# The triangular solver of a delta-rule layer on GpSimd instead of VectorE, with its indirect stores and mask in another order

## The reference

```python
A = jnp.where(tri, 0.0, -jnp.einsum('bhncd,bhnmd->bhncm', kb, k))
for i in range(1, chunk):
    A = A.at[..., i, :i].add(jnp.einsum('...j,...jk->...k', A[..., i, :], A[..., :, :i]))
T = A + jnp.eye(chunk, dtype=A.dtype)
u = T @ v
w = T @ kb
```

## Time and profile before

| | |
|---|---|
| executions, us | 1947.97, 1953.59, 1953.81 (median 1953.59) |
| profiled execution, first to last instruction, us | 2024.9 |
| TensorE busy | 1565.2 us, 77% |
| VectorE busy | 1359.5 us, 67% |
| ScalarE busy | 949.4 us, 47% |
| GpSimd busy | 446.7 us, 22% |
| mean granted TensorE clock | 0.879 of full speed |

### The profile page before, as it was taken

How to read it: one execution, slowest core, us unless ns; L and a number is a source line. 1 busy time by engine, 2 the same in 40 slices (tenths; PEclk the granted TensorE clock), 3 DMA queues, 4 the chain that set the end, 5 groups by cost and what they waited for, 6 DMA issues and landing times. The chain is left out here.

```text
span 2024.9 us, 40883 instructions
## 1 busy us (share of the span) xinstructions
PE 1565.2 (77%) x12507; PEld 1125.9 (56%) x12508; DVE 1359.5 (67%) x3875; ACT 949.4 (47%) x1990; POOL 446.7 (22%) x473
## 2 busy tenths in 40 slices
PE   6775258789988879989889889887445999999900
PEld 3455036557547548557458458366234777777700
DVE  7994164777867867867867867867446444444478
ACT  6761242454644644545445455442443444444434
POOL 6782200000130210210310310300314333333300
PEclk9997676999989989998999999978757999999955
DMA  6558722123323323333323332323514533333295
GB/s 203 187 171 225 168 42 51 34 59 94 85 73 95 98 60 96 98 82 91 90 63 98 90 88 83 86 61 84 189 63 136 188 95 95 96 96 95 79 340 204
DMA packets 297373, 224.36 MB, mean 111 GB/s; under 512 B 173472, under 2 KB 265632, under 8 KB 296960
## 3 DMA queue, kind: packets, MB, share of 16 engines
q1 hardware_dynamic: 225600, 158.84, 27.6%
q0 software_dynamic: 15232, 43.53, 6.0%
q10 hardware_dynamic: 56384, 19.93, 4.1%
HBM read 130.42 MB, written 91.82 MB: 110 GB/s over the span
## 5 line engine op out<-in xcount | busy, mean ns | idle before, releaser
L2035 POOL DMA_INDIRECT y_d<-C_yb,C_dest x136 | 131.6, 968 | 259.8 <-ACT C_yb L2146 257.2
L1459 DVE SCALAR_TENSOR_TENSOR B_conv<-B_ps_x,B_cw,B_conv 128x511 f32<-128x511 f32 (+2 forms) x192 | 143.9, 749 | 43.2 <-ACT B_conv L1177 38.2
L688 POOL MEMSET B_z<- 128x256 f32 (+4 forms) x40 | 6.3, 214 | 723.6 <-DMA B_z<-scr_a 723.6
L422 POOL DMA_INDIRECT xs_d<-x,slot_u x128 | 133.2, 1041 | 132.3 <-DVE m_acc L1861 95.5
L2271 DVE TENSOR_TENSOR C_xt_low<-C_ps_x,C_xt_high 128x256 fp32r<-128x256 f32 x136 | 57.8, 425 | 109.2 <-ACT C_xt_high L2130 109.1
L2265 DVE TENSOR_TENSOR C_av<-C_sg,C_ps_g 128x256 f32<-128x256 f32 x136 | 57.3, 421 | 95.5 <-ACT C_sg L2140 92.3
L2069 PE MATMUL C_ps_g<-C_w_high,C_xt_high 128*128 x272 | 119.5, 439 | 0.4 <-issue 0.4
L745 PE MATMUL B_ps_x<-B_xa,B_wk 128*128 128x512 f32 x128 | 68.4, 662 | 66.2 <-DVE B_sel L1451 45.0
L1177 ACT ACTIVATE B_conv<-B_ps_x,B_cw 128x512 f32<-128x512 f32 x64 | 43.7, 684 | 158.4 <-PE B_ps_x L745 157.0
L2069 PE MATMUL C_ps_g<-C_w_high,C_xt_low 128*128 x272 | 107.8, 396 | 0.0
L2069 PE MATMUL C_ps_g<-C_w_low,C_xt_high 128*128 x272 | 107.0, 393 | 0.0
(11 more groups left out here) (333 smaller groups left out, 4357.3 us busy)
## 6 DMA issues: line engine op xcount, KB each, us to landing
C_xb<-xs_d SPq DMA_DIRECT2D x136, 132.0 KB, 2.1
C_w_high<-y_d SPq DMA_DIRECT2D x12, 1024.0 KB, 14.1
A_band<-fir_long POOLq DMA_DIRECT2D x32, 256.0 KB, 5.9
A_work<-xT SPq DMA_DIRECT2D x16, 512.0 KB, 5.0
v_d<-A_v_tok SPq DMA_DIRECT2D x16, 512.0 KB, 3.4
short_d<-A_sh_tok SPq DMA_DIRECT2D x16, 512.0 KB, 3.1
B_xa<-xT SPq DMA_DIRECT2D x8, 1024.0 KB, 5.9
B_v_tok<-v_d SPq DMA_DIRECT2D x8, 1024.0 KB, 5.6
```

What stands on the lines that cost most here:

```text
L422: pool.indirect_dma_start(t["xs_d"][:, :], bass.IndirectOffsetOnAxis(ap=slot_u[:, c:c + 1], axis=0), x1[:, b, j, :], None).then_inc(done, 16)
L1459: V.scalar_tensor_tensor(conv[:, g % 2, k:], X[g % 2][:, :SEQ - k], cw[:, g // 4, gg % CH, 3 - k:4 - k], conv[:, g % 2, k:], ALU.mult, ALU ...
L2035: pool.indirect_dma_start(t["y_d"][:, :], bass.IndirectOffsetOnAxis(ap=dest[:, q:q + 1], axis=0), yb[:, u], None).then_inc(y_out[u], 16)
```

## The change

Three things change in stage B. The solver's 60 `tensor_tensor` go from VectorE to GpSimd, and the fills of the upper triangle from GpSimd to VectorE, which afterwards waits for both and makes the turned copy. GpSimd's step becomes solver, mask, stores. On all three engines the four groups of A stand in one row: TensorE runs `project(p, 6)` after the last of them, ScalarE and VectorE evict four times before they go on.

```diff
@@ GpSimd
-                def fill_blocks(p):
...
+                def solver(p):
+
+                    hold(pool, z_in, 64 * (p + 1))
+                    need(pool, x_out, 16 * p)
+                    need(pool, xt_out, 16 * p)
+                    k = SOLVE * p
+                    for j in range(1, BLK - 1):
+                        left = BLK - 1 - j
+                        need(pool, solve, k)
+                        pool.tensor_tensor(zt[:, 0:left, 0:j], z[:, j + 1:, j:j + 1].to_broadcast([P, left, j]),
+                                           z[:, j:j + 1, 0:j].to_broadcast([P, left, j]), ALU.mult).then_inc(solve, 1)
+                        pool.wait_ge(solve, k + 1)
+                        pool.tensor_tensor(z[:, j + 1:, 0:j], z[:, j + 1:, 0:j], zt[:, 0:left, 0:j], ALU.add).then_inc(solve, 1)
+                        k += 2
...
-                fill_blocks(0)
+                solver(0)
                 mask_at(0)
 
                 def step(i, has_prev, has_next):
                     if has_next:
-                        fill_blocks(i + 1)
+                        solver(i + 1)
+                        mask_at(i + 1)
                     if has_prev:
                         scatter(i - 1)
-                    if has_next:
-                        mask_at(i + 1)
@@ TensorE, stage1b
-                    project(p, 6)
                     for jj in range(2, 4):
                         for k in a_kept:
                             pe.wait_ge(k, 4 * p + jj - 1)
                         a_products(p, jj)
+                    project(p, 6)
@@ ScalarE, stage1b
-                    for jj in range(2):
+                    for jj in range(4):
                         keep_odd(jj)
                     group_b(p, 4)
                     if last is not None:
                         keep_routes(last)
                     group_a(p, 6)
-                    for jj in range(2, 4):
-                        keep_odd(jj)
@@ VectorE, stage1b and after it
-                    for jj in range(2):
+                    for jj in range(4):
                         keep_even(jj)
                     if not first:
                         late_rows(p - 1)
-                    for jj in range(2, 4):
-                        keep_even(jj)
...
-                def solver(p):
+                def fill_blocks(p):
...
+                def turn_solved(p):
+                    hold(dve, solve, SOLVE * (p + 1))
+                    hold(dve, masked, FILLS * (p + 1))
                     V.tensor_copy(zt[:], z[:].rearrange("p i k -> p k i")).then_inc(zt_ok, 1)
...
-                        solver(i + 1)
+                        fill_blocks(i + 1)
+                        turn_solved(i + 1)
```

More of the change, by code:

```diff
@@ L1515, in stage1b @@
                         place(last)
-                def solver(p):
+                def fill_blocks(p):
+                    whole = z[:]
                     hold(dve, z_in, 64 * (p + 1))
[L1520 to L1525, removed]
-                        V.tensor_tensor(zt[:, 0:left, 0:j], z[:, j + 1:, j:j + 1].to_broadcast([P, left, j]),
-                                        z[:, j:j + 1, 0:j].to_broadcast([P, left, j]), ALU.mult).then_inc(solve, 1)
-                        dve.wait_ge(solve, k + 1)
-                        V.tensor_tensor(z[:, j + 1:, 0:j], z[:, j + 1:, 0:j], zt[:, 0:left, 0:j], ALU.add).then_inc(solve, 1)
-                        k += 2
-                    dve.wait_ge(solve, SOLVE * (p + 1))
-                    dve.wait_ge(masked, FILLS * (p + 1))
+                    for k in range(FILLS - 1):
+                        half = BLK >> (k + 1)
+                        above = bass.AP(whole.tensor, whole.offset + half,
+                                        [whole.ap[0], [2 * half * (BLK + 1), 1 << k], [BLK, half], [1, half]])
+                        V.memset(above, 0.0).then_inc(masked, 1)
+                    diagonal = bass.AP(whole.tensor, whole.offset, [whole.ap[0], [BLK + 1, BLK]])
+                    V.memset(diagonal, 1.0).then_inc(masked, 1)
+                def turn_solved(p):
+                    hold(dve, solve, SOLVE * (p + 1))
+                    hold(dve, masked, FILLS * (p + 1))
                     V.tensor_copy(zt[:], z[:].rearrange("p i k -> p k i")).then_inc(zt_ok, 1)
@@ L1865, in _ @@
                 stage1b(0, first=True)
-                solver(0)
+                fill_blocks(0)
+                turn_solved(0)
                 taps_of(1, 0)
```

## The result

The changed kernel takes 2028.13 us (median of 4 runs, 2027.27 to 2032.72), the kernel before beside it 1953.69: a ratio of 1.0402, interval 1.0377 to 1.0427. That is 74 us slower, where I had forecast 28. The sign and the range (1937 to 2035) held; the size was wrong by a factor of 2.7.

What follows compares the result with a forecast made beforehand. The chain from L898 through merges, recurrence and next stage1b was taken to bound the step, VectorE's solver just hidden under the gate. Seven steps' 19 us plus 9 for the first solver gave 1953.6 + 28 = 1982 us, range 1937 to 2035.

Steps and rivals of the forecast that it cites:

- the stalls: ScalarE's 71.1 us of remote waits in the gate work, taken to belong to the traced execution alone.
- Term 1: Four evictions in a row in stage B: gate starts 1.9 us later, blocks reach the solver 2.5 us sooner.
- Term 2: The solver's 30 products and 30 additions on GpSimd: 34.4 us a solver, with 27 and 43 kept as alternatives.
- Term 3: GpSimd's solver and VectorE's short operations block each other at SBUF: 1.5 us on the gate's start, 1.5 on the solver.
- The solver's end: In step 5 the solver was to end at 1174.8 us on GpSimd, against 1168.3 on VectorE.
- Term 4: Solved blocks landing 7.6 us after the solver's end delay L898 on TensorE by 2.7 us a step, 19 for seven.
- Term 5: The 16 stores moved behind the mask, beside the mix: costed at nothing, upper bound 2 us a step.
- Term 6: The solver ahead of step 0, with nothing over it: 9.4 us more, all on the path.
- The quick solver's: Rival: solver below 32 us and mask out of VectorE's way, TensorE bounds the step, about 1950 us; chance 0.13.
- The long solver's: Rival: past 32.4 us plus waits each solver microsecond delays L898; at 43.4 us the kernel takes 2049; chance 0.15.
- The stalls' rival: ScalarE's stalls are in every execution, from stores beside the gate; moving the stores gives 1939 us; chance 0.17.

Runs made afterwards that it cites:

- e9: The kernel before, unchanged, run again for a second traced execution: traced span 1953.0 us, median 1954.58 us, ratio 1.0003.
- e4: The changed kernel with the evictions split again as before, solver still on GpSimd and stores behind the mask: 2037.12 us, ratio 1.0439.
- e1: The kernel before with only the evictions' part of the change, solver still on VectorE and stores ahead of the mask: 1960.69 us, ratio 1.0043.
- e2: The kernel before with only the mask moved ahead of the indirect stores on GpSimd: 1954.16 us, ratio 0.9998.
- e3: The kernel before with only the solver on GpSimd and the fills on VectorE, evictions and solver-stores-mask order kept: 2064.2 us, ratio 1.0565.
- e5: The changed kernel with each of the solver's 60 operations cut to at most 6 columns, the rest left out: 1972.07 us, ratio 1.0111.
- e7: The changed kernel with every second product of the solver computed twice, 15 more operations a solver: 2094.04 us, ratio 1.0731.
- e13: The kernel before without its 4 passes of filling products on TensorE ahead of the wait for the solved blocks' store: 1952.91 us, ratio 1.0010.

## Why the prediction was right in sign and wrong in size

*What bounds the kernel, the stalls.* Right: e9's span of 1953.0 without remote waits shows that the timed executions have none. The base of 1953.6 stood.

*Term 1, evictions.* Forecast: gate 1.9 later, blocks 2.5 sooner. With the solver on GpSimd (e4 to after) the gate moves 3.2 later and the blocks 1.2 sooner (L898 to A plus A to gate or solver). Alone they cost 0.43%, 8 us, where 1.9 a step would be 13. The gate's start then doesn't matter, since the solver is longer than the gate's work.

*Term 2, the solver on GpSimd.* Right: 34.4 forecast, 35.5 measured alone ahead of step 0 (281.52 to 316.99) and 35.9 in the loop. A product takes 247 ns at 30 elements and 612 at 240, an addition 272 and 696. The Trainium skill (GPSIMD Engine Reference, "Elementwise — side-by-side cycle accounting") led to an estimate of 37, and the trace agrees within 5%: from those means I get 0.2 us fixed and 1.7 to 2.0 ns an element.

*Term 3, SBUF.* The solver is 0.4 longer beside other work than alone, not 1.5; the gate's start 0.6 later behind A than in e1. Too high, and small.

*The solver's end.* Forecast to move by 6.5 us (1168.3 to 1174.8). Against the L898 in front of it, it moved from 119.8 to 126.6, 6.8. Right, with errors that cancel: VectorE's solver takes 22.2 undisturbed, where I took 24.1 from the stalled step, so the solver grew by 13.7 and not by 11.9; and its start came 6.9 sooner (6.1 from L898 to A, 0.8 behind A), not 5.4. Some 2.8 of that 6.9, in the mean of five steps, is the clock that falls less in the mix and the recurrence, which was not in the sum; e4, with the evictions as before, comes from L898 to A 3.4 sooner than e9, and the evictions add 2.7.

*Term 4, from the solver to L898: the step that failed.* "I take 2.7 a step, 19 for seven", between 2.0 and 3.4. L898 moved 10.3. The 8.3 between 2.0 and 10.3, by the ledger:
- The hand-off, 2.0 with the 0.3 of the solver's end. I took 7.6 from the end to the landing, from a step in which ScalarE's loads of `xf` came 10 us behind SyncE's of `mt` because of the stalls. Undisturbed they go out together (893.01 and 894.24 after, 985.65 and 985.79 in e9), and even before the change L882 starts 9.6 behind the end, and in four of seven steps waits 0.5 to 1.5 us for the landing. So L882 moved by 7.8 where I had 5.8. "VectorE's solver is just hidden under the gate" was wrong: in those four steps it was on the chain already.
- The base, 2.9. "So an undisturbed L898 starts at 1187.3" took step 0's distance, which held 3.8 us of waiting for VectorE, beside the mask. From L882 to L898 an undisturbed loop step has 7.8, not 10.7. The forecast let a late solver hide in a wait that wasn't there.
- The clock, 3.4. TensorE, idle for 3.4 and 5.0 us, runs the rows behind at the lower level, 1.2 GHz (granted 0.64 over the 7 us ahead of L899): 10.3 from L882 to L898 where I had 6.9. That a new wait costs the clock was not in the sum; nor that much of it comes back later, as the 2.8 above.

*Term 5, stores.* Right (e2), with the proviso of e3. The 2 us by which I had the stores slow VectorE's solver belonged to the stalled step: e9's takes 22.1 beside them. *Term 6, the first solver.* 9.4 forecast, 9.5 measured.

*The rivals.* The quick solver's falls with e5: at 26 us it still lost 1.1%. The long solver's mechanism was the true one (each microsecond of the solver is one on L898; e7), but at 36 us and not from 43. The stalls' rival fell with e9.

## What to carry to other kernels

Take all distances of a base step from the same undisturbed execution: here a gate from step 0 and a hand-off from a stalled step were each plausible, and together hid some 5 us that no step could hide. When a traced span and the timed runs disagree by 3%, trace again before counting slack. And when a chain lengthens, ask of the engine that will wait whether the rows behind the wait still run at the same clock, and where its clock fell until now, since that loss may only move.

## What the runs showed of the hardware

- The TensorE clock's slow stretch is moved by idling: in three of five loop steps e13 has a fall right ahead of L898 (0.63 in the one shown) and 1.00 where e9 has 0.77 and 0.87, at the same total time. The same rows behind L882 take 3.6 and 2.2 us.
- One traced execution held 71 us of ScalarE waits that a second trace (span 1953.0) doesn't have and for which the timed runs leave no room. What made them isn't known.
- GpSimd and VectorE on SBUF: a weighing of 1.22 us took 4.85 beside a mask of 3.87 (e5), nearly the two together. The Trainium skill (SBUF — State Buffer, "Who interferes with whom") has the lock that way, and the trace agrees; but the short operations of a solver cost their neighbours little (the gate's start behind A is 18.6 after and 18.0 in e1).
